# The end of a fused attention and feed-forward kernel, written out per engine, with other PSUM banks for the last batch

## The chip, the core and the metric

The kernel runs on one core of a Trainium2 chip. Five engines work side by side and meet only at semaphores: TensorE (PE, matrix products into PSUM), VectorE (DVE), ScalarE (ACT), GpSimd (POOL) and SyncE (SP, which here issues every DMA). PSUM has eight banks of 128 partitions by 512 float32. The metric is the device time in microseconds (us); lower is better. Three runs of the kernel before took 366.59, 366.3 and 364.39 us, with a median of 366.3 us. The profiled execution took 366.19 us, of which its span, from first to last instruction, is 364.5 us.

## What is computed

The input is 16 batches of 256 tokens of 256 features. Each token is normalised. Attention and a feed-forward network both read the normalised tokens, and both results are added to the input:

```python
xn = _layernorm(x)
x = x + attention(xn, w_qkv, w_out) + ffn(xn, w_gating, w_linear)
# attention: 16 heads of 16, causal
qkv = xn @ w_qkv                      # 256 x 768
scores = einsum('bqhd,bkhd->bhqk', q / 4, k)
attn = softmax(where(causal, scores, -1e10))
out = einsum('bhqk,bkhd->bqhd', attn, v) @ w_out
# ffn, operands in fp8: (gelu(xn @ wg[0]) * (xn @ wg[1])) @ w_linear
```

## The kernel before

The first part of the program runs normalisation and the feed-forward network. It leaves the input plus the feed-forward result in `xres`. The second part is attention, one batch after another, and the change touches only this part.

For a batch b the attention goes through these steps. Six units of heads, n = 0 to 5, are made of two halves c = 0 (n 0 to 2) and c = 1 (n 3 to 5).

- `max_scores` (PE) computes scores with queries on the partitions, and `find_max` (DVE, L457) takes each row's maximum. The scores lie in three banks, `max_ps`, in rotation.
- `transpose_max(b, c)` (PE, L814) turns the maxima of a half into rows, `negate_max` (ACT, L565) copies them with a minus sign, and `place_max` (SP, L231) sends them by DMA into the operand `stack`.
- `exp_scores(b, n)` (PE, L786) computes the scores again with keys on the partitions and the maximum already subtracted, into the two banks of `exp_ps`. `exponent(b, n)` (ACT, L572) takes the exponential of both banks into `arena`. Unit n may only be written once the exponential of unit n-1 has been read: `pe.wait_ge(exp_done, unit)`.
- `mask(b, n)` (POOL, L330) zeroes what lies above the diagonal.
- `times_v(b, c)` (PE, L805) multiplies by the values into the bank `pv_ps`, 32 small matmuls. It waits for the three masks of its half and for the half before it to have left the bank (`o_norm_done`).
- `o_to_rows` (DVE, L466) transposes the bank, and `normalize_o` (DVE, L472, L474, L481) divides by the sum of the exponentials and transposes back into `ot_raw`.
- `round_ot` (ACT, L581) rounds that to its high part, and `split_ot` (POOL, L335) subtracts to get the low part, counted by `ot_lo`.
- `project_out(b, c)` (PE, L822) multiplies by `w_out`, 6 matmuls for each half, into bank `misc[:, 0]`. `add_x(b)` (DVE, L487) adds `xres` and writes `y`, and `store_y(b)` (SP, L236) stores it.

The order on each engine is written out by hand as a loop over stages s, and several batches are under way at once: in stage s, PE does the maxima of batch s, the exponentials of batch s-1, `times_v` of batches s-2 and s-1 and `project_out` of batch s-3. The loops go on past the last batch, with `has(b)` leaving out steps of batches that don't exist. So the end of the program (stages 16 to 18) is the same order with most of its steps missing. Stage 16 on PE is, for instance: `exp_scores(15, 0)`, `transpose_max(15, 1)`, `exp_scores(15, 1)`, `exp_scores(15, 2)`, `times_v(14, 1)`, `exp_scores(15, 3)`, `project_out(13, 0)`, `exp_scores(15, 4)`, `project_out(13, 1)`, `exp_scores(15, 5)`, `times_v(15, 0)`. Stage 17 is `times_v(15, 1)` and `project_out(14, ...)`, and stage 18 is `project_out(15, ...)`, which waits until `add_x(14)` has read the same bank (`y_done`).

## Time and profile before

| quantity | value |
| --- | --- |
| median of three runs | 366.3 us (364.39 to 366.59) |
| profiled execution | 366.19 us, span 364.5 us |
| PE busy | 341.3 us (94% of the span) |
| DVE busy | 298.5 us (82%) |
| ACT busy | 227.6 us (62%) |
| POOL busy | 168.2 us (46%) |
| PE in the chain that ended last | 81% |
| mean granted TensorE clock | 0.972 |

Busy shares are means over the whole span. The stages of attention in which every batch is present and the last 23 us, in which batches run out, have different limits. So the end is read by itself, from the chain that ended last, from the engines' instructions in order of time, and from the granted clock in short stretches. A clock of 1.00 is the higher of TensorE's two levels (2.4 GHz), and 0.50 is the lower (1.2 GHz).

### The profile page before, as it was taken

How to read it: one execution, taken by the hardware profiler on the slowest of the kernel's cores; microseconds unless marked ns; L12 is line 12 of the kernel's file. 1: busy time of each engine (PE TensorE's matmuls, PEld its weight loads, DVE VectorE, ACT ScalarE, POOL GpSimd, SP SyncE). 2: the span in 40 equal slices, each digit the busy share in tenths (PEclk: the TensorE clock that was granted, in tenths of full speed). 3: DMA queues.
4: the chain of work that ended last, by engine and by line, in shares of the span. 5: the costliest groups of instructions: out<-in, count | busy, mean ns of one | idle time of the engine just before them, and what ended most of it. 6: DMA issues, size and time to landing. Idle time of an engine off the chain costs nothing.

```text
span 364.5 us, 9751 instructions
## 1 busy us (share of the span) xinstructions
PE 341.3 (94%) x3498; PEld 260.1 (71%) x3498; DVE 298.5 (82%) x1356; ACT 227.6 (62%) x368; POOL 168.2 (46%) x204
## 2 busy tenths in 40 slices
PE   7789999999999789999999999999999999979775
PEld 6336565666677678788788888888887888866454
DVE  5968988998425678999989999999999899996643
ACT  1655786667655376776676767766766767664540
POOL 2212333232235137456665575475566555753441
PEclk9969999999999999999999999999999999995889
DMA  7987655773248242534637528447355373250001
GB/s 251 323 287 224 183 151 141 175 232 123 77 142 298 65 145 90 201 120 150 193 112 225 167 97 263 120 144 246 104 179 195 112 222 118 91 206 30 32 29 59
DMA packets 46553, 57.59 MB, mean 158 GB/s; under 512 B 2664, under 2 KB 39080, under 8 KB 46504
## 3 DMA queue, kind: packets, MB, share of 16 engines
q1 hardware_dynamic: 46504, 56.96, 48.6%
q8 instruction: 28, 0.46, 0.5%
q14 instruction: 21, 0.17, 0.1%
HBM read 16.78 MB, written 12.58 MB: 81 GB/s over the span
## 4 chain that ended last, share of the span: by engine, by line
PE 81%; DVE 10%; ACT 3%; issue 2%; DMA 2%; SPq 0%; POOL 0%; DVEq 0%; ACTq 0%; POOLq 0%
PE ps L805 13%; PE ps L710 12%; PE ps L786 12%; PE ps L765 9%; PE ps L717 7%; PE ps L697 6%; PE ps L676 6%; PE ps L822 6%; PE ps L682 6%; DVE masked L457 3%; PE ps L814 2%; DMA xres<-in_L_attn_x_dram 2%; PE ps L661 2%; ACT arena L572 2%; DVE act L423 1%
## 5 line engine op out<-in xcount | busy, mean ns | idle before, releaser
L457 DVE CUSTOM_DVE_ANT_0 masked<-ps,causal 128x256 bf16<-128x256 f32 (+1 forms) x512 | 148.5, 353 | 21.1 <-PE ps L765 21.1
L572 ACT ACTIVATE arena<-ps 128x1024 f32<-128x1024 f32 x96 | 98.4, 1025 | 61.1 <-PE ps L786 61.0
L330 POOL TENSOR_SCALAR_AFFINE_SELECT arena<-arena 128x512 f32<-128x512 f32 (+1 forms) x96 | 73.6, 787 | 39.1 <-ACT arena L572 38.9
L304 POOL TENSOR_TENSOR qk_part<-w_raw,qk_part 128x512 fp32r<-128x512 f32 x32 | 41.1, 1286 | 55.5 <-ACT qk_part L551 55.5
L527 ACT ACTIVATE gate<-ps 128x512 bf16<-128x512 f32 x64 | 38.5, 602 | 35.0 <-PE ps L676 32.6
L786 PE MATMUL ps<-stack 64*128 64x256 f32 (+1 forms) x512 | 53.0, 307 | 4.8 <-ACT arena L572 4.8
L805 PE MATMUL ps<-arena,v_aug 128*32 128x256 f32 (+1 forms) x1024 | 50.8, 341 | 2.9 <-DVE o_norm L474 2.8
L710 PE MATMUL ps<-xs,wq_part 128*128 128x256 f32 x384 | 52.3, 285 | 0.3 <-ACT w_raw L545 0.3
L765 PE MATMUL ps<-stack 63*128 63x256 f32 (+1 forms) x512 | 48.3, 288 | 3.2 <-DVE row_max L457 3.1
L786 PEld LDWEIGHTS ps<-stack 64*128 64x128 f32 x512 | 36.9, 190 | 18.7 <-issue 7.3
L710 PEld LDWEIGHTS ps<-xs,wq_part 128*128 128x128 f32 x384 | 47.5, 189 | 1.6 <-ACT w_raw L545 0.6
L805 PEld LDWEIGHTS ps<-arena,v_aug 128*32 128x32 f32 x1024 | 30.1, 113 | 19.4 <-issue 6.0
L457 DVE DVE_READ_ACCUMULATOR2_ANT row_max<- 128x1 f32 x512 | 42.3, 83 | 0.0
L765 PEld LDWEIGHTS ps<-stack 63*128 63x128 f32 x512 | 37.4, 191 | 6.9 <-DVE row_max L457 2.4
L298 POOL TENSOR_TENSOR xres<-xres,ffn 128x512 f32<-128x512 f32 x16 | 18.5, 1154 | 37.6 <-ACT ffn L533 37.6
L423 DVE TENSOR_TENSOR arena<-ps,gate 128x512 fp8e4<-128x512 f32 x32 | 22.0, 686 | 16.0 <-ACT gate L527 15.9
L335 POOL TENSOR_TENSOR xt_part<-xn,xt_part 128x256 fp32r<-128x256 f32 x32 | 23.4, 731 | 22.9 <-ACT xt_part L581 22.9
L822 PE MATMUL ps<-wq_part,xt_part 128*128 128x256 f32 x192 | 31.4, 302 | 1.0 <-DVE w_raw L487 1.0
L466 DVE STREAM_TRANSPOSE ps<-ps 128x512 f32<-128x512 f32 x32 | 23.4, 731 | 8.0 <-PE ps L805 8.0
L822 PEld LDWEIGHTS ps<-wq_part,xt_part 128*128 128x128 f32 x192 | 25.5, 195 | 3.8 <-DVE w_raw L487 1.2
L423 DVE TENSOR_TENSOR act<-ps,gate 128x512 fp8e4<-128x512 f32 x32 | 21.9, 684 | 7.2 <-ACT gate L527 4.4
L717 PE MATMUL ps<-wq_part,xs 128*128 128x256 f32 x192 | 26.7, 288 | 0.0
(60 smaller groups left out, 458.6 us busy)
## 6 DMA issues: line engine op xcount, KB each, us to landing
stack<-qk_part SPq DMA_DIRECT2D x96, 256.0 KB, 2.7
xt_store<-xt_part SPq DMA_DIRECT2D x16, 512.0 KB, 4.2
xs<-xt_store SPq DMA_DIRECT2D x16, 512.0 KB, 4.2
out_dram<-w_raw SPq DMA_DIRECT2D x16, 256.0 KB, 4.1
xres<-in_L_attn_x_dram SPq DMA_DIRECT2D x7, 512.0 KB, 6.7
arena<-in_L_ffn_w_gating_dram SPq DMA_DIRECT2D x2, 1024.0 KB, 8.9
stack<-zeros SPq DMA_DIRECT2D x4, 512.0 KB, 7.5
arena<-in_L_ffn_w_linear_dram SPq DMA_DIRECT2D x1, 1024.0 KB, 12.9
```

The lines of the kernel that those rows point to most:

```text
L304: nc.gpsimd.tensor_tensor(qk_part[:, g, QLO:KLO + 1:3, :], qk_raw[:, g, :, :], qk_part[:, g, QHI:KLO, :].bitcast(F32), ALU.subtract).then_ ...
L330: nc.gpsimd.affine_select(diag, diag, pattern=[[0, 1024 // width], [1, P]], compare_op=ALU.is_ge, fill=0.0, base=0, channel_multiplier=-1) ...
L423: nc.vector.tensor_tensor(act8[c % 2][:, j, :], up_ps[j % 2], gate[:, j % 2, :], ALU.mult, saturate=False).then_inc(act_done, 1)
L457: last = nc.vector.tensor_tensor_reduce(masked[:, place, i * width:(i + 1) * width], max_ps[:, place, i * width:(i + 1) * width], causal[: ...
L527: nc.scalar.activation(gate[:, j % 2, :], gate_ps[j % 2], ACT.Gelu_apprx_tanh).then_inc(gelu_done, 1)
L572: nc.scalar.activation(arena[:, n, :, :], exp_ps, ACT.Exp).then_inc(exp_done, 1)
L710: last = nc.tensor.matmul(misc[:, 1, s * S:(s + 1) * S], wq_part[:, a, kt, col:col + P], xs[b % 2][:, z, kt, :], start=(i == 0), stop=(i = ...
L717: last = nc.tensor.matmul(misc[:, 0, t * D:(t + 1) * D], xs[b % 2][:, z, kt, t * P:(t + 1) * P], wq_part[:, a, kt, 2 * D:3 * D], start=(i ...
L765: last = nc.tensor.matmul(max_ps[:, (2 * unit + u) % 3, i * width:(i + 1) * width], st[rows, j0 + i, 0, qt * P:(qt + 1) * P], st[rows, j0 ...
L786: last = nc.tensor.matmul(exp_ps[:, u, i * width:(i + 1) * width], st[rows, j0 + i, 1, kt * P:(kt + 1) * P], st[rows, j0 + i, 0, kt * P:S] ...
L805: last = nc.tensor.matmul(pv_ps[32 * i:32 * i + 32, u * S + kt * P:(u + 1) * S], va[:, kt, 2 * (HG * c + i) + u, :], cols, start=(kt == 0) ...
L822: last = nc.tensor.matmul(misc[:, 0, t * D:(t + 1) * D], ot_part[:, z, c, t * P:(t + 1) * P], wq_part[:, a, c, 3 * D:4 * D], start=(c == t ...
```

## The change

Each engine's loop now ends with the last batch's stage (s = 15), and what came after it is written out as a list of its own. In that list:

- For batch 15, units 2 and 4 of `exp_scores` go into two banks of the maxima (`exp_banks`), which are free once all maxima are taken. So units 2 to 5 wait for the exponential two units back, not for the one before.
- `times_v(15, 0)` writes the third bank of the maxima (`pv_bank`), and waits for no `o_norm_done`. `transpose_max(15, 1)` writes `misc[:, 1]`. `project_out(15, ...)` writes the two banks of `exp_ps` (`y_bank`) and needs `exp_done` of all units, not `y_done`.
- `project_out(13, ...)` stands on each side of `transpose_max(15, 1)`, and `times_v(14, 1)` before `exp_scores(15, 2)`. `times_v(15, 0)` and `project_out(14, 0)` stand before `exp_scores(15, 5)`.
- POOL does `mask(14, 5)` and `split_ot(13, 1)` before `mask(15, 0)`. ACT does `round_ot(13, 1)` before `exponent(15, 0)`, and `round_ot(14, 0)` before `exponent(15, 3)`.
- The low part of the very last half is subtracted on DVE, behind `add_x(14)`, not on POOL. The last `add_x` and the last store are each in two halves of 128 tokens.

The names with `_last` and `out_ready` in the diff are new semaphores. Line numbers in the lists below are those of each kernel's own file.

PE from the end of stage 15 to `times_v(15, 0)`, before. `stack` with 128x128 is a unit 0 or 3 of the exponentials, `stack` with 128x256 the other units (4 matmuls each), `row_max` the transposed maxima, `v_aug` is `times_v` (four rows for one call), and `wq_part` is `project_out`:

```order
L786 MATMUL ps<-stack 128x128 x8
L814 MATMUL ps<-ident,row_max 8x128 x2
L786 MATMUL ps<-stack 128x256 x8
L805 MATMUL ps<-arena,v_aug 32x256 x4
...
L786 MATMUL ps<-stack 128x128 x8
L822 MATMUL ps<-wq_part,xt_part 128x256 x6
L786 MATMUL ps<-stack 128x256 x4
L822 MATMUL ps<-wq_part,xt_part 128x256 x6
L786 MATMUL ps<-stack 128x256 x4
L805 MATMUL ps<-arena,v_aug 32x256 x4
```

The same place of the changed kernel (L849 is `exp_scores`, L880 `transpose_max`, L871 `times_v`, L892 `project_out`):

```order
L849 MATMUL ps<-stack 128x128 x8
L892 MATMUL ps<-wq_part,xt_part 128x256 x6
L880 MATMUL ps<-ident,row_max 8x128 x2
L892 MATMUL ps<-wq_part,xt_part 128x256 x6
L849 MATMUL ps<-stack 128x256 x4
L871 MATMUL ps<-arena,v_aug 32x256 x4
...
L849 MATMUL ps<-stack 128x256 x4
L849 MATMUL ps<-stack 128x128 x8
L849 MATMUL ps<-stack 128x256 x4
L871 MATMUL ps<-arena,v_aug 32x256 x4
```

The twelve matmuls of `project_out(13, ...)` moved from among units 3 to 5 to the place before unit 1, and `times_v(14, 1)` moved ahead of unit 2.

POOL's last steps, before, from `mask(15, 0)` and `mask(14, 5)` on (`128x1024` is the mask of unit 0 or 3, `128x4x128` that of another unit; L335 is `split_ot`):

```order
L330 AFFINE_SELECT arena<-arena 128x1024
L330 AFFINE_SELECT arena<-arena 128x4x128
L335 TENSOR_TENSOR xt_part<-xn,xt_part 128x256
L330 AFFINE_SELECT arena<-arena 128x4x128 x2
L330 AFFINE_SELECT arena<-arena 128x1024
L330 AFFINE_SELECT arena<-arena 128x4x128
L335 TENSOR_TENSOR xt_part<-xn,xt_part 128x256
L330 AFFINE_SELECT arena<-arena 128x4x128
L335 TENSOR_TENSOR xt_part<-xn,xt_part 128x256 x3
```

And in the changed kernel (L349 is `mask`, L354 `split_ot`):

```order
L349 AFFINE_SELECT arena<-arena 128x4x128
L354 TENSOR_TENSOR xt_part<-xn,xt_part 128x256
L349 AFFINE_SELECT arena<-arena 128x1024
L349 AFFINE_SELECT arena<-arena 128x4x128 x2
L354 TENSOR_TENSOR xt_part<-xn,xt_part 128x256
L349 AFFINE_SELECT arena<-arena 128x1024
L349 AFFINE_SELECT arena<-arena 128x4x128 x2
L354 TENSOR_TENSOR xt_part<-xn,xt_part 128x256 x2
```

`mask(14, 5)` and `split_ot(13, 1)` now stand first, and one `split_ot` is gone from POOL.

The diff of the parts spoken of:

```diff
--- before.py
+++ after.py
...
@@ -139,6 +138,21 @@
         ot_ready, ot_hi, ot_lo, ot_used = sem("ot_ready"), sem("ot_hi"), sem("ot_lo"), sem("ot_used")
         y_done = sem("y_done")
         y_stored = [sem(f"y_stored{i}") for i in range(2)]
+        ot_lo_last, out_ready, y_last = sem("ot_lo_last"), sem("out_ready"), sem("y_last")
+
+        def exp_banks(b, n):
+
+            return max_ps[:, 0:2, :] if b == B - 1 and n in (2, 4) else exp_ps
+
+        def pv_bank(b, c):
+            return max_ps[:, 2, :] if b == B - 1 and c == 0 else pv_ps
+
+        def maxt_bank(b, c):
+            return misc[:, 1, :] if b == B - 1 else misc[:, 1 - c, :]
+
+        def y_bank(b, t):
+
+            return exp_ps[:, t, 0:D] if b == B - 1 else misc[:, 0, t * D:(t + 1) * D]
 
         block = ctx.enter_context(nc.Block())
 
@@ -232,8 +246,13 @@
                              neg_max[c][:, :].bitcast(F32)).then_inc(neg_in[c], 16)
 
             def store_y(b):
-                sp.wait_ge(y_done, b + 1)
-                sp.dma_start(out_tiles[b], y[b % 2][:, :, :]).then_inc(y_stored[b % 2], 16)
+                if b == B - 1:
+                    for t in range(QT):
+                        sp.wait_ge(y_last, t + 1)
+                        sp.dma_start(out_tiles[b][:, t, :], y[b % 2][:, t, :]).then_inc(y_stored[b % 2], 16)
+                else:
+                    sp.wait_ge(y_done, b + 1)
+                    sp.dma_start(out_tiles[b], y[b % 2][:, :, :]).then_inc(y_stored[b % 2], 16)
 
             sp.wait_ge(xt_stored, 16 * (B - 6))
             load_xs(0)
...
@@ -352,8 +371,17 @@
                     mask(s - 1, 4)
                 if has(s - 2):
                     split_ot(s - 2, 0)
-                if has(s):
+                if s < B - 1:
                     mask(s, 0)
+            mask(B - 2, 5)
+            split_ot(B - 3, 1)
+            for n in range(3):
+                mask(B - 1, n)
+            split_ot(B - 2, 0)
+            for n in range(3, UNITS):
+                mask(B - 1, n)
+            split_ot(B - 2, 1)
+            split_ot(B - 1, 0)
 
         @block.vector
         def _(dve):
@@ -463,11 +491,11 @@
             def o_to_rows(b, c):
 
                 dve.wait_ge(pv_ready, 2 * b + c + 1)
-                nc.vector.transpose(o_by_q, pv_ps).then_inc(o_by_q_done, 1)
+                nc.vector.transpose(pv_bank(b, c), pv_bank(b, c)).then_inc(o_by_q_done, 1)
 
             def normalize_o(b, c):
                 done = 2 * b + c + 1
-                o = o_by_q.rearrange("p (k e) -> p k e", e=2 * DH)
+                o = pv_bank(b, c).rearrange("p (k e) -> p k e", e=2 * DH)
                 dve.wait_ge(o_by_q_done, done)
                 nc.vector.reciprocal(r_den[:, :], o[:, :, DH]).then_inc(den_done, 1)
                 dve.wait_ge(den_done, done)
...
@@ -509,6 +537,23 @@
                 if has(s - 3):
                     add_x(s - 3)
 
+            find_max(B - 1, 5)
+            o_to_rows(B - 2, 0)
+            normalize_o(B - 2, 0)
+            add_x(B - 3)
+            o_to_rows(B - 2, 1)
+            normalize_o(B - 2, 1)
+            for c in range(2):
+                o_to_rows(B - 1, c)
+                normalize_o(B - 1, c)
+            add_x(B - 2)
+            dve.wait_ge(ot_hi, 2 * B)
+            nc.vector.tensor_tensor(ot_part[:, 1, 1, :], ot_raw[:, 1, :], ot_part[:, 0, 1, :].bitcast(F32), ALU.subtract).then_inc(ot_lo_last, 1)
+            dve.wait_ge(y_stored[1], 16 * (B // 2 - 1))
+            for t in range(QT):
+                dve.wait_ge(out_ready, t + 1)
+                nc.vector.tensor_tensor(y[1][:, t, :], y_bank(B - 1, t), xres[:, (B - 1) * QT + t, :], ALU.add).then_inc(y_last, 1)
+
         @block.scalar
         def _(act):
             def cast_xt(c, k):
@@ -562,14 +607,14 @@
                 act.wait_ge(maxt_ready[c], b + 1)
                 if b >= 1:
                     act.wait_ge(neg_in[c], 16 * b)
-                nc.scalar.mul(neg_max[c][:, :], misc[0:PAIRS, 1 - c, 0:S], -1.0).then_inc(neg_done[c], 1)
+                nc.scalar.mul(neg_max[c][:, :], maxt_bank(b, c)[0:PAIRS, 0:S], -1.0).then_inc(neg_done[c], 1)
 
             def exponent(b, n):
                 act.wait_ge(exp_ready, UNITS * b + n + 1)
                 if b >= 1 and n % 3 == 0:
 
                     act.wait_ge(pv_ready, 2 * (b - 1) + n // 3 + 1)
-                nc.scalar.activation(arena[:, n, :, :], exp_ps, ACT.Exp).then_inc(exp_done, 1)
+                nc.scalar.activation(arena[:, n, :, :], exp_banks(b, n), ACT.Exp).then_inc(exp_done, 1)
 
             def round_ot(b, c):
                 act.wait_ge(ot_ready, 2 * b + c + 1)
...
@@ -645,10 +690,22 @@
                     exponent(s - 1, 5)
                 if has(s + 2):
                     copy_qk(s + 2, 0)
-                if has(s):
+                if s < B - 1:
                     exponent(s, 0)
                 if has(s + 2):
                     round_qk(s + 2, 0)
+
+            round_ot(B - 3, 1)
+            exponent(B - 1, 0)
+            negate_max(B - 1, 1)
+            exponent(B - 1, 1)
+            exponent(B - 1, 2)
+            round_ot(B - 2, 0)
+            for n in range(3, UNITS):
+                exponent(B - 1, n)
+            round_ot(B - 2, 1)
+            for c in range(2):
+                round_ot(B - 1, c)
 
         @block.tensor
         def _(pe):
@@ -775,7 +832,13 @@
                 if unit == 0:
 
                     pe.wait_ge(ffn_done, 2 * CHUNKS)
-                if unit >= 1:
+                if b == B - 1 and n in (2, 4):
+                    pe.wait_ge(max_done, 2 * UNITS * B)
+                    if n == 4:
+                        pe.wait_ge(exp_done, unit - 1)
+                elif b == B - 1 and n in (3, 5):
+                    pe.wait_ge(exp_done, unit - 1)
+                elif unit >= 1:
                     pe.wait_ge(exp_done, unit)
                 heads, kt = (4, 1) if n % 3 == 0 else (2, 0)
                 width = 512 // heads
@@ -783,7 +846,7 @@
                 for i in range(heads):
                     for u in range(2):
                         rows = slice(64 * u, 64 * u + ROW + 1)
-                        last = nc.tensor.matmul(exp_ps[:, u, i * width:(i + 1) * width],
+                        last = nc.tensor.matmul(exp_banks(b, n)[:, u, i * width:(i + 1) * width],
                                                 st[rows, j0 + i, 1, kt * P:(kt + 1) * P], st[rows, j0 + i, 0, kt * P:S],
                                                 start=True, stop=True)
                 last.then_inc(exp_ready, 1)
@@ -793,7 +856,10 @@
                 pe.wait_ge(p_masked[c], 3 * (b + 1))
                 if c == 0:
                     pe.wait_ge(v_done, b + 1)
-                if 2 * b + c >= 1:
+                if b == B - 1:
+
+                    pe.wait_ge(*((max_done, 2 * UNITS * B) if c == 0 else (o_norm_done, 2 * b)))
+                elif 2 * b + c >= 1:
                     pe.wait_ge(o_norm_done, 2 * b + c)
                 for u in range(2):
                     for kt in range(QT):
@@ -802,7 +868,7 @@
                                 cols = arena[:, 3 * c + 1 + i // 2, u, i % 2 * S:(i % 2 + 1) * S]
                             else:
                                 cols = arena[:, 3 * c, u, i * P:(i + 1) * P]
-                            last = nc.tensor.matmul(pv_ps[32 * i:32 * i + 32, u * S + kt * P:(u + 1) * S],
+                            last = nc.tensor.matmul(pv_bank(b, c)[32 * i:32 * i + 32, u * S + kt * P:(u + 1) * S],
                                                     va[:, kt, 2 * (HG * c + i) + u, :], cols,
                                                     start=(kt == 0), stop=(kt == QT - 1), tile_position=(0, 32 * i),
                                                     skip_group_check=True)
@@ -811,21 +877,28 @@
             def transpose_max(b, c):
                 pe.wait_ge(max_done, 2 * UNITS * b + UNITS * (c + 1))
                 for t in range(QT):
-                    last = nc.tensor.transpose(misc[0:PAIRS, 1 - c, t * P:(t + 1) * P],
+                    last = nc.tensor.transpose(maxt_bank(b, c)[0:PAIRS, t * P:(t + 1) * P],
                                                row_max[:, b % 2, t, PAIRS * c:PAIRS * (c + 1)], ident[:])
                 last.then_inc(maxt_ready[c], 1)
 
             def project_out(b, c):
-                pe.wait_ge(ot_lo, 2 * b + c + 1)
+                if 2 * b + c < 2 * B - 1:
+                    pe.wait_ge(ot_lo, 2 * b + c + 1)
+                else:
+                    pe.wait_ge(ot_lo_last, 1)
                 for t in range(QT):
+                    first = c == 0 and (t == 0 or b == B - 1)
                     for i, (a, z) in enumerate(((0, 0), (0, 1), (1, 0))):
-                        last = nc.tensor.matmul(misc[:, 0, t * D:(t + 1) * D], ot_part[:, z, c, t * P:(t + 1) * P],
-                                                wq_part[:, a, c, 3 * D:4 * D], start=(c == t == i == 0), stop=(c == 1 and i == 2),
+                        last = nc.tensor.matmul(y_bank(b, t), ot_part[:, z, c, t * P:(t + 1) * P],
+                                                wq_part[:, a, c, 3 * D:4 * D], start=(first and i == 0), stop=(c == 1 and i == 2),
                                                 skip_group_check=True)
-                last.then_inc(ot_used, 1)
+                    if b == B - 1 and c == 1:
+                        last.then_inc(out_ready, 1)
+                if not (b == B - 1 and c == 1):
+                    last.then_inc(ot_used, 1)
 
             pe.wait_ge(gelu_done, J * CHUNKS)
-            for s in range(B + 4):
+            for s in range(B):
                 if has(s - 1):
                     exp_scores(s - 1, 0)
                 if has(s):
@@ -885,6 +958,27 @@
                     max_scores(s, 5)
                 if has(s - 1):
                     times_v(s - 1, 0)
+
+
+            exp_scores(B - 1, 0)
+            pe.wait_ge(y_done, B - 3)
+            project_out(B - 3, 0)
+            pe.wait_ge(neg_done[0], B)
+            transpose_max(B - 1, 1)
+            project_out(B - 3, 1)
+            exp_scores(B - 1, 1)
+            times_v(B - 2, 1)
+            for n in range(2, 5):
+                exp_scores(B - 1, n)
+            times_v(B - 1, 0)
+            pe.wait_ge(y_done, B - 2)
+            project_out(B - 2, 0)
+            exp_scores(B - 1, 5)
+            times_v(B - 1, 1)
+            project_out(B - 2, 1)
+            pe.wait_ge(exp_done, UNITS * B)
+            project_out(B - 1, 0)
+            project_out(B - 1, 1)
 
 
 # ---- launch: one core; inputs and outputs as the reference has them ----
```

## Rows read from the trace of the kernel before

**Rows 1.** The page: span, PE, and slices of the granted clock.
```profile
span 364.5 us, 9751 instructions
PE 341.3 (94%) x3498; PEld 260.1 (71%) x3498; DVE 298.5 (82%) x1356; ACT 227.6 (62%) x368; POOL 168.2 (46%) x204
PEclk9969999999999999999999999999999999995889
```

**Rows 2.** Chain that ended last, from 341.45 us: start, length, engine and line.
```profile
341.45 0.61 PE ps L786 x8
...
342.08 1.03 ACT arena L572
...
343.16 0.52 PE ps L786 x4
...
345.40 2.72 PE ps L805 x32
...
352.12 1.48 PE ps L805 x32
...
355.26 1.54 PE ps L805 x32
...
359.41 1.70 PE ps L822 x12
...
361.14 0.69 DVE w_raw L487
```

**Rows 3.** Timeline: start, length, engine, line, count, [idle before <-releaser].
```profile
339.29 1.02 ACT L572 ACTIVATE arena<-ps 128x1024 f32<-128x1024 f32 x1 [1.00 <-PE ps L786]
...
343.18 1.68 POOL L330 TENSOR_SCALAR_AFFINE_SELECT arena<-arena 128x1024 f32<-128x1024 f32 x2 [3.48 <-ACT arena L572]
...
344.78 0.63 PE L786 MATMUL ps<-stack 64*128 64x256 f32 x4 [1.12 <-ACT arena L572]
...
348.80 0.98 PE L822 MATMUL ps<-wq_part,xt_part 128*128 128x256 f32 x6
...
353.26 0.64 POOL L330 TENSOR_SCALAR_AFFINE_SELECT arena<-arena 128x512 f32<-128x512 f32 x1 [0.30 <-ACT arena L572]
...
358.34 0.45 DVE L481 STREAM_TRANSPOSE xn<-o_norm 128x256 f32<-128x256 f32 x1
358.71 0.65 DVE L487 TENSOR_TENSOR w_raw<-ps,xres 128x512 f32<-128x512 f32 x1
358.81 0.41 ACT L581 CAST xt_part<-xn 128x256 fp32r<-128x256 f32 x1 [0.65 <-DVE xn L481]
359.30 0.73 POOL L335 TENSOR_TENSOR xt_part<-xn,xt_part 128x256 fp32r<-128x256 f32 x1 [0.33 <-ACT xt_part L581]
```

**Rows 4.** Stretches: bounds, length, busy of PE to POOL, clock, DMA share, GB/s.
```profile
328.00:338.00 10.00, 9.14 (x74) 6.90 (x75) 6.38 (x37) 4.66 (x7) 3.16 (x5) 0.50 0.08 27
341.50:345.00 3.50, 1.64 (x16) 1.03 (x18) 2.50 (x10) 2.58 (x4) 1.68 (x2) 1.00 0.05 18
345.00:348.00 3.00, 3.00 (x36) 1.48 (x34) 0.00 (x0) 1.04 (x2) 1.95 (x3) 0.50 0.23 77
348.50:353.50 5.00, 4.57 (x60) 3.27 (x58) 2.24 (x5) 3.71 (x5) 2.66 (x4) 1.00 0.09 30
362.50:363.00 0.50, 0.00 (x0) 0.00 (x0) 0.00 (x0) 0.00 (x0) 0.00 (x0) 1.00 0.47 162
363.00:363.50 0.50, 0.00 (x0) 0.00 (x0) 0.00 (x0) 0.00 (x0) 0.00 (x0) 1.00 1.00 334
```

**Rows 5.** Single lines' durations (min/median/max ns), first and last start, shapes.
```profile
L414 DVE TENSOR_TENSOR wq_part<-w_raw,wq_part x8: 412/498/590, 41.7 to 77.8; 128x256 fp32r<-128x256 f32 x8
...
L474 DVE TENSOR_TENSOR o_norm<-ps,r_den x32: 424/425/426, 144.9 to 357.9; 128x256 f32<-128x256 f32 x32
```

**Rows 6.** Timeline at the first `place_max` and the first `exp_scores`, which waits for it.
```profile
123.53 6.62 SPq L231 DMA_DIRECT2D stack<-neg_max  x2
...
126.11 0.56 PE L786 MATMUL ps<-stack 64*128 64x128 f32 x8
```

More of the change, by code:

```diff
@@ L106, in attention_ffn @@
         max_ps, exp_ps, pv_ps, misc = ps[:, 0:3, :], ps[:, 3:5, :], ps[:, 5, :], ps[:, 6:8, :]
-        o_by_q = pv_ps
         gate_ps, up_ps = [max_ps[:, 0, :], max_ps[:, 1, :]], [max_ps[:, 2, :], pv_ps]
@@ L262, in _ @@
             for i in range(2):
-                sp.wait_ge(y_stored[i], 16 * (B // 2))
+                sp.wait_ge(y_stored[i], 16 * (B // 2 + i * (QT - 1)))
         @block.gpsimd
@@ L336, in split_ot @@
                                         ALU.subtract).then_inc(ot_lo, 1)
-            for s in range(B + 5):
+            for s in range(B):
                 if has(s - 2):
@@ L488, in add_x @@
                                         xres[:, b * QT:(b + 1) * QT, :], ALU.add).then_inc(y_done, 1)
-            for s in range(B + 3):
+            for s in range(B):
                 if has(s - 1):
@@ L617, in _ @@
             copy_ffn(CHUNKS - 2, 1)
-            for s in range(B + 4):
+            for s in range(B):
                 if has(s - 1):
```

2 lines of the change are left out of this document (1 added, 1 removed).

## The prediction

> **What bounds the kernel now.** I read the page first. PE is busy 94% of a span of 364.5 us, and the slices of the granted clock show 9 nearly everywhere, but 5, 8 and 8 close to the end [rows 1]. The change touches nothing before stage 16, so I went on to the chain that ended last, from the point where PE finishes `times_v(14, 0)` at 341.45 us, and read there which wait ends last. The chain alternates: `exp_scores(15, 0)` on PE, its exponential on ACT (1.03 us), the next 0.52 us of PE, and so on, since one pair of banks holds all scores; then `times_v(14, 1)` takes 2.72 us, where `times_v(15, 0)` takes 1.48 us for the same 32 matmuls; `times_v(15, 1)` starts at 355.26, the last `project_out` ends at 361.11 and the last `add_x` at 361.83 [rows 2]. The span ends 2.67 us later, with the store [rows 1, 2].
>
> The stretches explain the 2.72 us. Between 341.5 and 345.0 PE is busy 1.64 of 3.5 us at a clock of 1.00; from 345.0 to 348.0 it is busy throughout at 0.50, with no other engine's work in the way; from 348.5 it is back at 1.00 [rows 4]. So before the low stretch (1.2 GHz) PE had mostly waited for ACT, and the low stretch cost 2.72 - 1.48 = 1.24 us in `times_v(14, 1)` alone.
>
> **The change, part by part.** I walk the new order from 341.45 with durations of rows. Handoffs are 0.02 us from PE to ACT, 0.05 us from ACT to PE (342.08 + 1.03 to 343.16), 0.08 us from ACT to POOL (352.16 + 1.02, an exponential's length as in the row at 339.29, to 353.26) and about 0.15 us from DVE to PE [rows 2, 3]. The handoff from POOL to PE has no row of its own; I take 0.1 us, between 0.05 and 0.15.
>
> *PE up to unit 2.* `exp_scores(15, 0)` ends at 342.06. `project_out(13, 0)` follows at once: six matmuls are half of 1.70 us, 0.85, so to 342.91 [rows 2]. Its low part is an old one, split in stage 15. The transposed maxima take about 0.35, to 343.26, which is 0.5 us later than now. `project_out(13, 1)` to 344.11: it needs `split_ot(13, 1)`. Before, POOL sat idle 3.48 us and then did `mask(15, 0)` at 343.18 and `mask(14, 5)` behind it, though the exponential of (14, 5) was over at 340.31 [rows 3]. In the new order the mask and `split_ot(13, 1)` run at 340.4 to 341.8 (0.64 + 0.73), in that idle time, and `round_ot(13, 1)` (0.41) on an ACT that waits for PE. They cost nothing; without that cover they would put 1.4 us before PE's second `project_out`. Unit 1 takes 0.50, to 344.61. It was at 343.16, so it is 1.0 us late, but `times_v(14, 1)` then follows directly, at full clock, to 346.09, and unit 2 needs no exponential to finish, being in the banks of the maxima: to 346.6.
>
> *The late maxima.* `place_max(15, 1)` is issued behind a negation that ends at about 343.65. At its first use the DMA was issued at 123.53 and PE went on at 126.11, so at most 2.6 us pass [rows 6]. It has landed by 346.3, and unit 3 comes at 346.6. That leaves 0.3 us, and ACT is busy until 348.05 anyway. I cost it at nothing.
>
> *To `times_v(15, 1)`.* ACT does unit 2 from 346.62 to 347.65, then `round_ot(14, 0)` (0.41), unit 3 from 348.1 and unit 4 to 350.2. POOL masks unit 2 at 347.73 to 348.37. PE does `times_v(15, 0)` from 348.46 to 349.95, `project_out(14, 0)` to 350.8 (its `split_ot`, 0.73 after the mask, ends at 349.1) and unit 5 to 351.3. ACT 351.32 to 352.35, POOL's mask 352.43 to 353.07, so `times_v(15, 1)` starts at about 353.2. It started at 355.26: **2.1 us** earlier. Of these, 1.24 is the low clock and the rest is order and banks. What is late next is the chain unit 5, exponential, mask; `times_v(15, 1)` is queued behind it with `project_out(14, 1)` behind that.
>
> *The tail.* Before, from the start of `times_v(15, 1)` to the end of the last `add_x` there were 361.83 - 355.26 = 6.57 us [rows 2]. Now: 1.5 for `times_v`; then 1.99 up to the end of the last transpose (356.80 to 358.34 + 0.45, rows 2 and 3), which gives 356.7. ACT rounds in 0.41 to 357.1. DVE does `add_x(14)` first (0.65) and is free at 357.35. The subtraction then has no row of its own: the same shape from SBUF took 412 to 590 ns, mean 0.50, on this engine [rows 5]; I take 0.50, ends 0.41 and 0.59, against POOL's 0.73 [rows 3]. So 357.85, PE from 358.0, six matmuls 0.98 [rows 3] to 359.0, the second half of `add_x` in 0.42 as the nearest operation with 256 columns from PSUM took [rows 5] (0.65 as the upper end, the full row), to 359.4. That is 6.2 us in place of 6.57, **0.35 us** won. `project_out(14, 1)` and `project_out(15, 0)`, 1.7 us, lie under the 3 us of DVE and ACT work, because they no longer wait for `add_x(14)` to leave the bank; before, 1.70 us of PE stood after it [rows 2].
>
> *The store.* The last one moved its bytes from about 362.75 to 363.5 at up to 334 GB/s [rows 4]. The last half is 128 KB: half of the 0.75 us, **0.35 us** less (0 if the fixed part rules, and 0.4 at most). The first half's issue on SP lies under the second `add_x`.
>
> The Trainium skill's page VectorE: DVE Perf Modes (section on the TRN2 errata, SBUF-src ops) gives 58 + 256 cycles at 0.96 GHz for the subtraction, an estimate of 0.33 us. By it the sum would be 0.17 us better; the rows of this kernel, 0.41 at the least, speak against it, so the sum keeps the row.
>
> **Sum:** 2.1 + 0.35 + 0.35 = 2.8 us off. The profiled execution took 366.19 us, 0.1 below the median of 366.3, so I expect **363.4 us**. With the ends of the unknown terms it is 362.7 to 364.2 at the same clock.
>
> **Rivals.**
>
> *The low clock moves instead of going.* PE now works 341.45 to 346.6 without a gap, where before it waited most of the time, which is why I drop the low stretch. Against that: from 328 to 338 PE was busy 9.14 of 10 us and the clock stayed at 0.50 [rows 4], so being busy is no sure cure. If the stretch comes back over `times_v(14, 1)` and units 2 and 3, it costs 1.24 us in `times_v` plus 0.4 us on units 2 and 3 (0.50 us on the path, at the same ratio 2.72 / 1.48 = 1.84): 2.8 - 1.6 = 1.2 off, 365.0 us (364.3 to 365.8). Also, the same place need not be low in every run of the kernel before (the runs spread by 2.2 us), in which case a part of my 1.24 us was never there to win, with the same result.
> The Trainium skill's page TensorE: Matmul & The Clock Gate (section on HAM oscillation) ties the fall to idle gaps of PE longer than any here. In this trace the clock fell at 345.0 although the longest gap just before was 1.12 us [rows 3], so the trace does not agree. By that rule the new order could not cure the stretch, and the time would be this rival's.
>
> *The end as a whole goes low: slower.* From 346.6 on the new order has new gaps on PE: about 0.3 us before unit 4, 1.9 us before `times_v(15, 1)`. If the clock falls there, `times_v(15, 0)`, `project_out(14, 0)`, unit 5 and `times_v(15, 1)`, 4.3 us of PE work on the path, cost 0.84 as much again, 3.6 us: 367.0 us. It decides from 3.3 us of such work on. For it: the fall at 345. Against: before, gaps of the same kind behind 353.6 left the clock at 1.00, and from 348.5 PE had 1.00 again, with the last slice at 9 [rows 1, 4].
>
> *More is won.* If the low stretch also costs units 2 and 3 and the exponentials behind them, and all the small terms fall at their low ends, 3.8 to 4.3 us go, 362.3 us.
>
> *It does nothing.* That would need the path to lie elsewhere, for instance in unit 3 waiting for its maxima by more than 3 us. With 0.3 us to spare and ACT covering 1.4 more, I give it little.
>
> **Chances.** Forecast 52%, low clock back 26%, more won 15%, slower 5%, nothing 2%. A measurement here tells a change of about 1% (3.7 us) from none. Faster by over 1% means below 362.6: all of the 15% and a few of the forecast's lower edge, 0.20. Slower by over 1% means above 370: part of the slower rival only, 0.02. The rest, 0.78, is within 1%. The range from 362.0 to 366.0 leaves out the slower rival, the far end of the winners and some of the second's upper edge, together under 2 in 10.
>
> **What would show it.** Right: in the profile after, `times_v(14, 1)` at about 1.5 us before unit 2; a clock of 1.00 between 345 and 348; `times_v(15, 1)` starting near 353.2; no PE wait for `place_max`; `project_out(15, 0)` done before DVE's subtraction; the last `add_x` ending near 359.4 and the store 2.3 us behind. Wrong: a slice of 0.50 in the end, `times_v(14, 1)` at 2.7 us, unit 3 released by a DMA, or unit 5 held back by `project_out(14, 0)` and its `split_ot`.

## The result and the profile after

The changed kernel took 363.15 us (median of 22 runs, 360.22 to 365.19), the kernel before 366.27 us (22 runs, 361.95 to 368.74). The ratio is 0.9936, with a 95% interval of 0.9914 to 0.9959. It leaves out slow executions, those over 1.5% above the fastest of the same kernel (four of the kernel before), so it is not the quotient of the two medians. That is less time by more than the noise, and by less than 1%: 3.1 us by the medians, 2.3 us (1.5 to 3.1) by the ratio. The profiled execution took 362.12 us, with a span of 360.3 us in place of 364.5 us. Of these 4.2 us, 0.8 lie in work that the change does not touch: `times_v(14, 0)` ended at 340.69 in place of 341.45. So I count from that end.

The page after, its first rows and its clock slices, to be held against [rows 1]:

```profile
span 360.3 us, 9754 instructions
PE 337.3 (94%) x3498; PEld 257.8 (72%) x3498; DVE 298.8 (83%) x1358; ACT 228.0 (63%) x368; POOL 167.5 (46%) x203
PEclk9989999999999999999999999999999999996798
```

The chain that ended last, from 340.69 us (start, length, engine and line; L849 is `exp_scores`, L871 `times_v`, L892 `project_out`, L617 the exponential, L349 `mask`, L551 the last subtraction, L555 the last add):

```profile
340.69 0.59 PE ps L849 x7
341.28 0.91 PE ps L892 x6
...
343.55 1.44 PE ps L871 x32
...
345.46 1.03 ACT arena L617
...
346.55 0.64 POOL arena L349
...
347.24 1.51 PE ps L871 x32
348.75 0.91 PE ps L892 x6
349.66 0.45 PE ps L849 x4
...
350.13 1.03 ACT arena L617
...
351.23 0.64 POOL arena L349
...
351.91 1.55 PE ps L871 x32
...
356.02 0.34 DVE xt_part L551
```

`times_v(14, 1)` is 1.44 us where it was 2.72, and only two exponentials are left on the path, where the chain before ran through four. Beside the one at 342.08 [rows 2] these were, in the trace before:

```profile
343.70 1.03 ACT arena L572
...
348.92 1.03 ACT arena L572
...
350.54 1.04 ACT arena L572
```

POOL's mask is now a link before each `times_v` of batch 15. `times_v(15, 1)` starts 11.22 us behind the end of `times_v(14, 0)`; it was 13.81.

The timeline shows the cover on POOL and PE's longest wait (start, length, engine, line, and idle time with what ended it):

```profile
339.61 0.64 POOL L349 TENSOR_SCALAR_AFFINE_SELECT arena<-arena 128x512 f32<-128x512 f32 x1 [0.68 <-ACT arena L617]
...
340.21 0.73 POOL L354 TENSOR_TENSOR xt_part<-xn,xt_part 128x256 fp32r<-128x256 f32 x1
...
351.91 1.51 PE L871 MATMUL ps<-arena,v_aug 128*32 128x256 f32 x32 [1.82 <-POOL arena L349]
...
355.37 0.65 DVE L515 TENSOR_TENSOR w_raw<-ps,xres 128x512 f32<-128x512 f32 x1
...
355.95 0.41 DVE L551 TENSOR_TENSOR xt_part<-xn,xt_part 128x256 fp32r<-128x256 f32 x1
...
356.41 0.98 PE L892 MATMUL ps<-wq_part,xt_part 128*128 128x256 f32 x6 [1.37 <-DVE xt_part L551]
...
357.14 0.76 DVE L555 TENSOR_TENSOR w_raw<-ps,xres 128x256 f32<-128x256 f32 x2 [0.79 <-PE ps L892]
```

And stretches, as [rows 4] (bounds, length, busy time of PE, PEld, DVE, ACT and POOL, granted clock, DMA share, GB/s):

```profile
327.00:337.00 10.00, 8.90 (x73) 6.66 (x74) 6.38 (x39) 4.64 (x7) 3.40 (x5) 0.51 0.09 28
341.00:344.50 3.50, 3.50 (x48) 2.86 (x50) 2.82 (x9) 2.31 (x3) 1.09 (x1) 1.00 0.05 18
344.50:347.50 3.00, 2.07 (x39) 1.39 (x32) 1.86 (x4) 2.16 (x4) 1.58 (x3) 1.00 0.48 161
347.50:352.50 5.00, 3.18 (x58) 2.21 (x53) 1.86 (x4) 2.74 (x5) 3.30 (x5) 1.00 0.00 0
```

PE was busy throughout the 3.5 us in which it had been busy 1.64, and the clock stayed at 1.00 behind them. The low stretch of 10 us in stage 15 is still there.

### The profile page after: what moved, and what is told of

Read it like the earlier page. It is cut to its first block, busy times and chain, and to the rows that moved or that the text cites. A ratio compares the mean times of both kernels' runs of the same rounds, so it can differ in the third digit from the quotient of the medians.

```text
span 360.3 us, 9754 instructions
## 1 busy us (share of the span) xinstructions
PE 337.3 (94%) x3498; PEld 257.8 (72%) x3498; DVE 298.8 (83%) x1358; ACT 228.0 (63%) x368; POOL 167.5 (46%) x203
## 4 chain that ended last, share of the span: by engine, by line
PE 80%; DVE 9%; DMA 4%; issue 2%; ACT 2%; POOL 1%; SPq 1%; DVEq 0%; ACTq 0%; POOLq 0%
PE ps L871 13%; PE ps L767 12%; PE ps L849 11%; PE ps L822 9%; PE ps L774 7%; PE ps L754 6%; PE ps L892 6%; PE ps L733 6%; PE ps L739 5%; DVE masked L485 3%; DMA xres<-in_L_attn_x_dram 3%; PE ps L880 2%; PE ps L718 2%; ACT arena L617 1%; DMA xt_store<-xt_part 1%
## 5 line engine op out<-in xcount | busy, mean ns | idle before, releaser
L617 ACT ACTIVATE arena<-ps 128x1024 f32<-128x1024 f32 x96 | 98.5, 1028 | 59.6 <-PE ps L849 59.5
L349 POOL TENSOR_SCALAR_AFFINE_SELECT arena<-arena 128x512 f32<-128x512 f32 (+1 forms) x96 | 73.6, 787 | 38.1 <-ACT arena L617 38.1
L849 PE MATMUL ps<-stack 64*128 64x256 f32 (+1 forms) x512 | 52.5, 305 | 3.6 <-ACT arena L617 3.6
L871 PE MATMUL ps<-arena,v_aug 128*32 128x256 f32 (+1 forms) x1024 | 49.5, 335 | 3.2 <-POOL arena L349 1.8
L849 PEld LDWEIGHTS ps<-stack 64*128 64x128 f32 x512 | 36.7, 190 | 16.9 <-issue 8.4
L871 PEld LDWEIGHTS ps<-arena,v_aug 128*32 128x32 f32 x1024 | 29.5, 111 | 19.1 <-issue 3.0
L892 PE MATMUL ps<-wq_part,xt_part 128*128 128x256 f32 x192 | 31.6, 302 | 1.4 <-DVE xt_part L551 1.4
L354 POOL TENSOR_TENSOR xt_part<-xn,xt_part 128x256 fp32r<-128x256 f32 x31 | 22.7, 732 | 18.7 <-ACT xt_part L626 18.7
L892 PEld LDWEIGHTS ps<-wq_part,xt_part 128*128 128x128 f32 x192 | 25.6, 195 | 4.2 <-DVE xt_part L551 1.6
```

The source lines that it names most:

```text
L349: nc.gpsimd.affine_select(diag, diag, pattern=[[0, 1024 // width], [1, P]], compare_op=ALU.is_ge, fill=0.0, base=0, channel_multiplier=-1) ...
L617: nc.scalar.activation(arena[:, n, :, :], exp_banks(b, n), ACT.Exp).then_inc(exp_done, 1)
L849: last = nc.tensor.matmul(exp_banks(b, n)[:, u, i * width:(i + 1) * width], st[rows, j0 + i, 1, kt * P:(kt + 1) * P], st[rows, j0 + i, 0, ...
L871: last = nc.tensor.matmul(pv_bank(b, c)[32 * i:32 * i + 32, u * S + kt * P:(u + 1) * S], va[:, kt, 2 * (HG * c + i) + u, :], cols, start=( ...
L892: last = nc.tensor.matmul(y_bank(b, t), ot_part[:, z, c, t * P:(t + 1) * P], wq_part[:, a, c, 3 * D:4 * D], start=(first and i == 0), stop ...
```

## The experiments

All kernels are read by one measure besides their time. **Stretch** is the time in the profiled execution from the end of `times_v(14, 0)` to the end of the last add; "start" is how far `times_v(15, 1)` starts behind the same point; "store" is from the last add to the end of the span. Stage 15 is from the start of `times_v(13, 0)` to that of `times_v(14, 0)`. The time is the median of all runs. The ratio is to runs of the kernel before taken beside the row's own: their median was 366.27 us for the second row, 365.8 for e1 to e4, 364.9 for e5 to e8, 365.98 for e9 and e10, and 366.16 for the two repeats. So rows of different groups are compared by ratio and not by time.

| kernel | time, us (runs) | ratio to before, 95% | stage 15 | start | stretch | store |
| --- | --- | --- | --- | --- | --- | --- |
| before | 366.27 (22) | 1 | 16.74 | 13.81 | 20.38 | 2.64 |
| changed | 363.15 (22) | 0.9936 [0.9914, 0.9959] | 16.75 | 11.22 | 17.21 | 2.38 |
| changed, again | 362.81 (10) | 0.9918 [0.9888, 0.9948] | 14.52 | 11.22 | 17.21 | 2.38 |
| e1: before, fillers in stage 16 | 363.56 (12) | 0.9968 [0.9932, 1.0003] | 14.65 | 12.24 | 18.82 | 2.64 |
| e2: changed, one pair of banks | 366.37 (10) | 1.0022 [0.9989, 1.0055] | 14.55 | 15.37 | 22.61 | 2.38 |
| e3: changed, one O bank | 364.39 (10) | 0.9981 [0.9953, 1.0009] | 14.43 | 11.22 | 17.21 | 4.31 |
| e3 again (e12) | 361.38 (9) | 0.9865 [0.9824, 0.9906] | 13.28 | 11.23 | 17.21 | 4.02 |
| e4: changed, old tail | 363.43 (10) | 0.9946 [0.9915, 0.9978] | 14.22 | 11.20 | 17.89 | 2.64 |
| e5: changed, fillers in stage 15 | 361.92 (12) | 0.9920 [0.9882, 0.9958] | 13.29 | 11.22 | 18.19 | 2.37 |
| e6: changed, exponentials first | 360.93 (10) | 0.9898 [0.9863, 0.9932] | 14.43 | 9.30 | 15.34 | 2.38 |
| e7: e5 and e6 | 360.23 (6) | 0.9896 [0.9852, 0.9941] | 13.28 | 9.31 | 15.36 | 2.37 |
| e8: before, second pair only | 365.72 (10) | 1.0015 [0.9976, 1.0054] | 14.67 | 14.41 | 20.99 | 2.64 |
| e9: e7, unit 2 earlier | 359.47 (6) | 0.9819 [0.9782, 0.9856] | 13.28 | 8.77 | 14.81 | 2.38 |
| e10: changed, old POOL order | 367.31 (10) | 1.0045 [1.0017, 1.0073] | 13.28 | 16.45 | 23.15 | 2.37 |

The stores come in two sizes: 2.64 us where the last store is one piece, 2.37 or 2.38 us where it is in halves, and more in the kernel of e3 and e12 alone. (The prediction had 2.67 us for the kernel before, from a span rounded to 0.1 us.)

The time carries stage 15 and all the work before it, which vary by more than 2 us between executions of the same code, while the stretch was the same to 0.01 us in two profiles of the changed kernel. So mechanisms are judged by the stretch, and whole kernels by the ratio. Neither is free of chance. Every stretch but the repeated ones comes from one profile, and e5, whose end is the changed kernel's to the letter, has 18.19 us in place of 17.21, because the clock fell there. And the ratio of one and the same kernel was 0.9981 in e3 and 0.9865 in e12, with intervals that do not touch: an interval covers the spread within one group, and not all of that between groups.

**e1, the clock by itself.** The kernel before, with matmuls that fill PE's waits:

```diff
@@ before, stage 16 on PE
+                    if s == B:
+                        pe.wait_ge(neg_done[0], B)
+                        fill(2)        # misc[:, 1] <- 128x128 times 128x256, unused
                     transpose_max(s - 1, 1)
+                    if s == B:
+                        fill(2)
...
                     exp_scores(s - 1, 1)
+                    if s == B:
+                        fill(7)
```

> The kernel before, with eleven extra full-array matmuls (0.14 us each) into a free bank in stage 16, where PE waits for ACT: 2 before transpose_max(15,1), 2 behind it, 7 behind exp_scores(15,1). Their results are not used. Theory A (the low clock behind 345 came from PE's waiting, and cost 1.2 to 1.6 us of the 3.1): the clock stays at 1.00 over times_v(14,1), which takes 1.5 us in place of 2.7, and from the end of times_v(14,0) to the end of the last add_x there are about 19.0 us in place of 20.4; time about 1.2 us under the kernel before. Theory B (the clock falls whatever PE does, and the gain is order and banks alone): times_v(14,1) stays at 2.7, the stretch at 20.4 us or a little over, time within 0.5 us of before.

Two stretches of this kernel, on either side of the start of `times_v(14, 1)`:

```profile
340.20:343.70 3.50, 3.17 (x27) 2.52 (x29) 2.50 (x10) 2.56 (x4) 1.68 (x2) 1.00 0.07 22
343.70:346.70 3.00, 3.00 (x50) 2.25 (x48) 1.13 (x3) 1.69 (x3) 1.95 (x3) 1.00 0.22 72
```

Where before had 1.64 of 3.5 us and then 0.50 [rows 4], this has 3.17 and then 1.00. The stretch fell by 1.56 us to 18.82, with nothing reordered. Theory A holds: this is what the low clock cost in the old order. It is made up of `times_v(14, 1)` (1.51 us where it was 2.79), unit 2 (0.50 where it was 0.63) and unit 3 (0.66 where it was 0.82). The ratio, 0.9968, agrees in sign, but its interval reaches just over 1.

**e2, the second pair of banks.** 

```diff
         def exp_banks(b, n):
-            return max_ps[:, 0:2, :] if b == B - 1 and n in (2, 4) else exp_ps
+            return exp_ps
...
+                if unit >= 1:
+                    pe.wait_ge(exp_done, unit)
```

> The changed kernel, with units 2 and 4 of the last batch's exp_scores back in exp_ps and each unit waiting for the exponential before it. If the second pair of banks carries a good part of the gain: unit 3 can start only when the exponential of unit 2 is over (about 5.8 us behind the end of times_v(14,0), not 4.8), unit 4 a whole exponential later (7.5), so times_v(15,0) starts 1.3 us later than in the changed kernel (7.9 in place of 6.55) and the time is 1.3 us over the changed kernel. If the pair is hidden behind times_v and project_out and order alone counts: no change, within 0.3 us, in the trace's stretch.

PE in this kernel (L843 `exp_scores`, L865 `times_v`), and its stretches:

```profile
345.95 0.66 PE L843 MATMUL ps<-stack 64*128 64x128 f32 x8 [1.21 <-ACT arena L617]
347.72 0.80 PE L843 MATMUL ps<-stack 64*128 64x256 f32 x4 [1.11 <-ACT arena L617]
348.45 2.79 PE L865 MATMUL ps<-arena,v_aug 128*32 128x256 f32 x32
...
355.37 2.79 PE L865 MATMUL ps<-arena,v_aug 128*32 128x256 f32 x32 [1.82 <-POOL arena L349]
```

```profile
343.50:347.00 3.50, 1.90 (x36) 1.21 (x24) 1.86 (x4) 2.10 (x4) 1.77 (x3) 1.00 0.44 150
347.00:360.00 13.00, 10.45 (x87) 7.02 (x88) 3.54 (x8) 3.31 (x5) 3.94 (x6) 0.50 0.00 1
```

Unit 3 comes 5.95 us and unit 4 7.7 us behind `times_v(14, 0)`, close to the 5.8 and 7.5 expected, but the loss is 5.4 us and not 1.3: the clock falls to 0.50 during the second of PE's two new waits (1.2 and 1.1 us), and stays there for 13.6 us, which slows everything on PE after it. Both theories missed the size. `times_v(15, 0)` starts 1.9 us later than in the changed kernel, of which 0.3 is unit 4 at half clock already; the other 3.5 us are matmuls at half clock, such as the two `times_v` of 2.79 us where the changed kernel has 1.51. This is one profile. By the ratios (1.0022 and 0.9936) the whole time rose by 0.9%, about 3 us.

**e3, the O bank.** `pv_bank` always `pv_ps`, with the old wait for `o_norm_done`.

> The changed kernel, with times_v(15,0) back in the bank pv_ps, waiting for normalize_o(14,1). By the changed kernel's trace normalize_o(14,1) has left the bank at 346.53, before times_v(15,0) starts at 347.24 for its mask, so both theories that name the exponentials as the path expect no change (stretch 17.2 us, within 0.15). If the O bank were a part of the gain, times_v(15,0) would wait on DVE and the stretch grow by 0.5 us or more.

The stretch is 17.21 us here and in e12: the third bank of the maxima brings nothing in this order. The store is another matter, below.

**e4, the tail.** One `y_bank` in `misc` behind `add_x(14)`, the last `split_ot` on POOL, one add, one store.

> The changed kernel with the tail as it was: project_out(15) in misc and behind add_x(14), the last split_ot on POOL, one last add_x, one last store. By the traces' own terms (6.57 to 5.99 us from the start of times_v(15,1) to the last add, 2.67 to 2.4 us behind it) the tail is worth 0.85 us: start of times_v(15,1) unchanged at 11.2 us behind times_v(14,0), then 6.6 us, then 2.7 us. If the tail's parts hide each other (PE's earlier project_out under the same DVE chain), the loss is under 0.4 us.

The loss is 0.68 us in the stretch and 0.26 us in the store, 0.94 us in all, with the start unchanged. About 0.1 us of it is the clock, which fell at 355.8, inside the last `project_out` (1.80 us, where the kernel before had 1.69). The ratios (0.9946 and 0.9936) can't tell a difference of this size.

**e8, the banks in the old order.** The kernel before, with `exp_banks` and its waits alone.

> The kernel before with the second pair of banks for units 2 and 4 of the last batch, in the old order, and nothing else of the change. If the banks carry the gain: unit 2 of the exponentials comes 0.6 us sooner, the later units no longer alternate with ACT, times_v(15,1) starts 1 to 2 us sooner behind times_v(14,0) than 13.8 us, and the stretch is 18.5 to 19.3 us. If the order is what matters (times_v(14,1) still stands behind unit 2, at low clock): the stretch stays over 19.8 us.

```profile
341.66 0.74 PE L795 MATMUL ps<-stack 64*128 64x256 f32 x8 [0.40 <-ACT arena L575]
343.42 2.51 PE L814 MATMUL ps<-arena,v_aug 128*32 128x256 f32 x32 [1.01 <-POOL arena L333]
```

Unit 2, which in this form waits for the maxima and for no exponential, comes at once with unit 1 (x8), but `times_v(14, 1)` then waits 1.01 us for POOL, where `mask(14, 5)` stands behind `mask(15, 0)`, and the clock falls as before, for 6.8 us where the kernel before had 3.4. The stretch is 20.99 us, no better than before, as the second theory said. What one wait gives back the next one takes.

**e10, POOL's order.** 

```diff
+            mask(B - 1, 0)
             mask(B - 2, 5)
             split_ot(B - 3, 1)
-            for n in range(3):
+            for n in range(1, 3):
                 mask(B - 1, n)
```

> The changed kernel with mask(15,0) before mask(14,5) and split_ot(13,1) on POOL, as before the change. The prediction priced this cover at 1.4 us. By the changed kernel's trace mask(15,0) starts at 342.4 for its exponential, so mask(14,5) and split_ot(13,1) end at 344.9, and the second half of project_out(13), which stood at 342.2, waits until then: times_v(14,1) starts 5.5 us behind the end of times_v(14,0) in place of 2.8, and the stretch grows by 2 to 2.7 us (19.2 to 19.9). With a rival that PE has slack there: under 1 us.

PE (L893 `project_out`, L872 `times_v`):

```profile
342.48 1.65 PE L893 MATMUL ps<-wq_part,xt_part 128*128 128x256 f32 x6 [2.43 <-POOL xt_part L354]
344.06 0.79 PE L850 MATMUL ps<-stack 64*128 64x256 f32 x4
344.78 2.79 PE L872 MATMUL ps<-arena,v_aug 128*32 128x256 f32 x32
```

The wait of 2.43 us is close to what was worked out (from 342.2 to 344.9). The clock fell during it, which was not: `times_v(14, 1)` started 6.45 us behind in place of 5.5 and took 2.79, the clock fell once more at 355.4, behind PE's wait for the last mask, and the stretch grew by 5.9 us in place of 2 to 2.7. With this one order undone the changed kernel is slower than the kernel before, by 2.8 us of stretch in the profile and by a ratio of 1.0045 (interval above 1). From the changed kernel's 0.9936 that is 1.1%, about 4 us.

**e5, e6, e7: two versions to go further.** e5 puts `fill(6)` behind `transpose_max(14, 1)` and behind `exp_scores(14, 1)` in stage 15. e6 is this on PE, with ACT's and POOL's `round_ot(14, 0)` and `split_ot(14, 0)` moved behind the last exponential and mask:

```diff
-            for n in range(2, 5):
+            for n in range(2, UNITS):
                 exp_scores(B - 1, n)
             times_v(B - 1, 0)
+            times_v(B - 1, 1)
             pe.wait_ge(y_done, B - 2)
             project_out(B - 2, 0)
-            exp_scores(B - 1, 5)
-            times_v(B - 1, 1)
             project_out(B - 2, 1)
```

> The changed kernel with twelve extra full-array matmuls into a free bank in stage 15, where PE waits for DVE and ACT (6 behind transpose_max(14,1), 6 behind exp_scores(14,1)); their results are not used. In both kernels the clock falls to 0.50 between these two waits (327 to 328) and stays there for 10 us, times_v(13,1) taking 2.8 us. Theory A (PE's waits let the clock fall): the clock stays at 1.00 through stage 15, times_v(13,1) takes 1.5 us, and the time is 2 to 3 us under the changed kernel, about 361. Theory B (the fall there is of another cause, or DVE's maxima bound stage 15 anyway): the same low stretch, or a high one without a gain, within 0.5 us of the changed kernel.

> The changed kernel with unit 5 of the exponentials before times_v(15,0), project_out(14,0) behind times_v(15,1), and round_ot(14,0) and split_ot(14,0) behind the last exponential and mask. If unit 5, its exponential and its mask are the path to times_v(15,1), as the changed kernel's chain says: times_v(15,1) starts 9.7 to 9.9 us behind the end of times_v(14,0), not 11.2, and the stretch to the last add is 15.8 to 16.0 us, not 17.2; time about 1.3 us less. If ACT's chain of six exponentials or the O path through DVE binds instead: under 0.5 us. If the waits between the units make the clock fall as in the kernel with one pair of banks: 1.5 to 3 us more.

> The two changes together on the changed kernel: fillers in stage 15, and the exponentials first in the end. If both hold and add: 3.5 to 4 us under the changed kernel, about 359.5. If the gain of one is a clock that the other needs as well, they overlap and it is no better than the better of the two.

Three stretches of e5:

```profile
328.00:340.00 12.00, 10.68 (x136) 8.46 (x128) 11.61 (x71) 7.04 (x10) 7.56 (x11) 1.00 0.26 90
350.00:353.00 3.00, 1.18 (x14) 0.84 (x16) 1.62 (x4) 1.62 (x3) 1.30 (x3) 1.00 0.02 5
353.00:356.50 3.50, 3.50 (x37) 2.42 (x31) 1.01 (x3) 0.00 (x0) 1.17 (x2) 0.53 0.00 0
```

The clock held through stage 15, which took 13.29 us in place of 16.75, and it held there in e7 and e9 too. Yet the same stage took 14.2 to 14.7 us in seven profiles without fillers there, because the low stretch there was shorter, and 13.28 us in two (e10, e12) with no low stretch there at all. So fillers save what the execution would have lost, and that is mostly 1 us and not the 2 to 3 that I expected. The whole time does not show it: the ratios of e5 and the changed kernel, 0.9920 and 0.9936, are within each other's intervals. In this profile the clock then fell in the end instead, after PE's wait for the last mask, and `times_v(15, 1)` took 2.52 us. That is the slower rival of the prediction, in a mild form. Before the same wait, of 1.82 us, the clock held in the two profiles of the changed kernel and in e3, e4 and e12, whose code is the same up to there but for one bank, so in this order the fall is a matter of chance.

e6 did what the chain said: start 9.30, stretch 15.34 us, 1.9 us less than the changed kernel and a little more than expected. e7 adds up in the profile (13.28 and 15.36 us), but not in the time: expected were 3.5 to 4 us under the changed kernel, and its ratio of 0.9896, from six runs, is that of e6 (0.9898), about 1.5 us under.

**e9, the best version.** e7, with `exp_scores(B - 1, 2)` before `times_v(B - 2, 1)`.

> The kernel with fillers in stage 15 and the exponentials first, with unit 2 of exp_scores before times_v(14,1) too, so that ACT, which sat idle for 0.85 us between units 1 and 2, has it at once. If ACT's chain of exponentials is what sets the start of times_v(15,1) there: it starts 8.8 us behind the end of times_v(14,0) in place of 9.3, the stretch is 14.8 to 15.0 us in place of 15.35, and the time is 0.4 us less than without it, about 359.8. If unit 3 of PE, which needs its maxima by DMA, binds instead: no change.

Start 8.77, stretch 14.81 us, as worked out. At 359.47 us (ratio 0.9819, interval 0.9782 to 0.9856) it is the fastest kernel here, 1.8% under before, from six runs. It was not run beside the changed kernel or e7. The 0.8% between its ratio and that of e7 is more than the 0.55 us of stretch can explain, so a part of the 1.8% is spread between groups.

**e11 and e12, the changed kernel and e3 once more, on one chip.**

> The changed kernel once more, beside the next one on the same chip. Expected as before: about 3 us under the kernel before, stretch from the end of times_v(14,0) to the last add 17.2 us, 2.4 us from the last add to the end of the span.

> The changed kernel with times_v(15,0) back in pv_ps, once more. Its first trace had the same stretch as the changed kernel, 17.2 us, but 4.3 us from the last add to the end, with a 16 KB transfer of instructions beside the last store, and its median was 1 us more. If that transfer falls there by the program's layout: 4.3 us again and 1 to 2 us over the changed kernel beside it. If it was chance: about 2.4 us at the end and within 0.5 us of the changed kernel.

The changed kernel repeats. For e12, SP's longest waits (engine and line, waited for: total, times, longest):

```profile
SPq L255 <- DVE w_raw L515: 10.3, 1, 10.3
SPq L282 <- DMA out_dram<-w_raw: 3.0, 1, 3.0
```

The last store landed late again, 3.0 us of waiting where the changed kernel has 1.4, so in the profiled executions this is no chance. But e12's time was 1.4 us less than that of the changed kernel beside it, not 1 to 2 more. Its profile shows where that came from: the clock never fell before 352.7 us, and `times_v(14, 0)` ended at 335.69 us, 4 us sooner than in e11, which had low stretches at 135 and in stage 15. That is no property of its code that I can name. Whether the late store exists in the other executions stays open.

## Why the prediction was right

The forecast was 363.4 us and the measured median 363.15, in the range, and within 1% as its largest chance said. That it is this near is partly luck. In the profiles the end gained 3.4 us where the sum had 2.8, the whole time gained 2.3 us by the ratio, and two executions of the same code can differ by more than either. What stands is the mechanism. By its own steps:

- **The clock term (1.24 us).** The forecast's mechanism is shown, by e1: PE's waiting before 345 brought the low stretch, and filling it brought it back to 1.00. Its size was 1.56 us, since units 2 and 3 ran in part at half clock as well. In the changed kernel `times_v(14, 1)` took 1.5 us at 1.00. I had held back because PE was busy for 9.14 of 10 us at 0.50 from 328 to 338 [rows 4]. That is what a stretch did that was low already. Where the clock was at 1.00 and PE was busy for 3.50 us (changed) or 3.17 us (e1) of the next 3.5, it stayed there. Whether the term was there in every execution, which the prediction doubted, no run shows. The mean clocks of the last section show only that low stretches come and go.
- **The walk to `times_v(15, 1)` (2.1 us).** Measured: 2.6 us. All links were there in the order walked. The start was 0.5 us early, mostly because I added whole durations (0.35 for the transposes, 0.85 for the second half of `project_out`, 0.50 for a unit, 1.48 for `times_v`) where the chain shows increments of 0.22, 0.71, 0.43 and 1.44: neighbours overlap on PE.
- **POOL's cover (costed at nothing).** `mask(14, 5)` at 339.61 and `split_ot(13, 1)` at 340.21 lay in idle time. The price of losing that cover, given as 1.4 us, was mis-sized: e10 has a wait of 2.43 us and 5.9 us in the stretch, since POOL also does the mask of unit 0 first and the clock falls during the wait.
- **The late maxima (nothing).** No PE wait for that DMA shows; unit 3 ran with unit 2 from 344.92.
- **The tail (0.35 us) and the store (0.35 us).** 0.58 and 0.26 us in the traces. e4, with the tail undone, gives 0.68 and 0.26. The subtraction took 0.41 us, the low end of its range, and began before `add_x(14)` was recorded as over.
- **The subtraction's price.** The sum rightly kept to the rows: the measured 0.41 us is the least of [rows 5]. The Trainium skill's figure (VectorE: DVE Perf Modes, section on the TRN2 errata) gave an estimate of 0.33 us, which the trace does not bear out.
- **The rivals.** That the low stretch moves did not happen in the changed kernel's two profiles before its last add. In e2, e5, e8 and e10 the clock did fall in the end, at PE waits of 1.0 to 2.4 us; in the kernel before, the longest gap ahead of the fall at 345 was 1.12 us [rows 3]. The Trainium skill (TensorE: Matmul & The Clock Gate, section on HAM oscillation) ties the fall to idle gaps of PE longer than any in these traces, so they do not agree with it.
- What I did not see is that the parts need each other. I priced them one by one as a sum. e8 (banks without order) is worth nothing, and e2 and e10 (one part taken away) cost 5.4 and 5.9 us of stretch in their profiles, more than the 3.2 us that the whole change gains there.

## What to carry to other kernels

At the end of a pipeline, where steps run out, write the order out anew: find the last chain, then give every other engine the work that the chain will need before it needs it, POOL's queue order as much as the banks. Price a wait on PE by its length and by the matmuls behind it at half clock; the waits of e2 and e10, 2.3 and 2.4 us, cost 5.4 and 5.9 us in their profiles. And judge a change of 1% by a stretch in the trace that starts behind the noise, since 22 whole times of the same code here spread by 5 us. Take that stretch more than once: one fall of the clock in it was worth 1 us in e5.

## What the runs showed of the hardware

The low clock in stage 15 lasted about 10 us in two profiles (before and changed), 3.4 us in seven, and was absent in two without fillers there, for the same order of work up to there: stage 15 took 16.7, 14.2 to 14.7, and 13.28 us. A single profile gives the size of such a stretch, not its mean.

Most of the spread between executions goes with the clock. Ninety-nine executions of the kernel before ran beside the experiments. Three of them, at a mean granted clock of 0.995, took 361.8 to 362.1 us; 27 at 0.986 took 363.6 to 365.3; 30 at 0.977 took 365.1 to 367.8; and four at 0.958 took 370.5 to 371.2. A mean of 0.995 over 360 us leaves at most 3.6 us at 0.50, so in those three the low stretches of stage 15 (10.3 us) and of stage 16 (3.4 us) that the profile shows were not both there.

The last store of 128 KB landed 3.8 us (e3) and 3.5 us (e12) after its issue in the two profiles of one kernel, against 1.8 us in the other kernels with that store; the half before it took 2.0 us, against 1.7. A 16 KB transfer of instructions ran beside the stores of these two, and not of the changed kernel's. The trace of e8 has the same pair: such a transfer at 359.14 ran beside the store of batch 14, issued at 358.50, which landed after 3.6 us, while the same store took 2.1 us in the kernel before and in e1 without a transfer beside it. So in all three traces in which such a transfer fell among the last stores, a store landed late. That one causes the other was not tested.
